# Second experts: gate and up products from half-precision high and low parts, and the routing weights spread by one product

## The chip, the cores and the metric

One core of a Trainium2 chip runs the whole program. The metric is the time of one execution on the device in microseconds (us). TensorE multiplies matrices, VectorE (DVE) and ScalarE (ACT) do elementwise work out of PSUM and SBUF, GpSimd (POOL) does elementwise work on SBUF, SyncE (SP) issues the DMAs. Each has its own queue of instructions and they meet at semaphores.

## The reference

Two layers on x of 8 x 256 tokens of 128 numbers, each a cross attention and an expert layer. Cut to what the change touches, the last expert layer:

```
logits = xf @ gate_weight.T                 # xf: 2048 x 128 (layer-normed), 32 experts
scores = sigmoid(logits)
... # 4 of 8 groups by their best score + bias, then the 6 best experts of those
combine = scores of the 6 / their sum * 2.5, else 0        # 2048 x 32
def expert_step(acc, inp):                  # for each of 32 experts
    gu, dn, c = inp
    g = xf @ gu[:I].T                       # I = 64
    u = xf @ gu[I:].T
    o = silu(g) * u @ dn.T
    return acc + c[:, None] * o
shared = (silu(xf @ shared_gate_w.T) * (xf @ shared_up_w.T)) @ shared_down_w.T     # 128 wide
x = x + tanh(g_ffn[1]) * (routed + shared)
```

Every token goes through every expert with the weight `combine`, which is zero for most.

## The kernel before

The program is a row of blocks, each with a queue per engine written out by hand; a block ends when all its engines have. Nothing is ordered by a scheduler. The last three are the second attention, `block_route1` and the product loop of `block_experts1`. The attention isn't changed, but is where rows for operations like the new ones come from.

`block_route1` (L1783): SyncE issues the loads of the router's weights and bias, and then, by `load_experts` (L1903), those of gate, up and down weights and of `spread`, all on one queue. VectorE norms x, TensorE turns it (L780), ScalarE and VectorE copy the turned x from PSUM to `xT` (L1829, L1838), TensorE makes the logits (L1822), ScalarE the sigmoid (L1831). The routing that follows is a chain of 38 VectorE instructions from L1842 to L1879, each waiting for the one before; the last writes `combine`. GpSimd has nothing in this block.

`block_experts1` (L1882): two experts of 64 make one pair of 128 columns; 16 pairs and the shared expert make N = 17 turns. TensorE turns `combine` into PSUM (L1922), ScalarE casts it to half precision `c_hi` (L1962), VectorE takes the rest into `c_lo` (L1974). Then for each of four stretches of 512 tokens ("a pass") and each turn p:

- `up(blk, p)`: gate product (L1934) and up product (L1935), both in float, and the turn's routing weights spread over its 128 columns by two half-precision products, 33 rows of `c_hi` (L1937) and 32 rows of `c_lo` (L1938) against `spread`. Three PSUM banks a turn, two sets of them.
- ScalarE: silu of the gate bank (L1968). VectorE: times the up bank (L1979), times the spread weights (L1986), which gives `inner`.
- `down(blk, p)`: four float products `inner` by down weights (L1947), added up in one bank over all 17 turns. At the end of a pass VectorE adds it to x (L1990).

Of the kernel before, what the change touches and what calls it, by code (L numbers as in the profile page):

```python
# [23 lines left out]
ACT = mybir.ActivationFunctionType  # L24
AX = mybir.AxisListType
F32 = mybir.dt.float32
F16 = mybir.dt.float16
# [3 lines left out]
P = 128  # L31
# [5 lines left out]
TOK = B * T  # L37
# [3 lines left out]
BANK = 512  # L41
# [10 lines left out]
F0 = 256  # L52
X1, I1 = 32, 64
PAIRS = X1 * I1 // P
GR, KEEP, TOP = 8, 4, 6
SCALE1 = 2.5
UB = H * TT
# [1727 lines left out]
                        query_lo(it + 3)  # L1785

def block_route1(nc, m, s, dram, load_experts):

    normed, turned, xt_act, xt_dve = (s.sem(f"r1_{n}") for n in ("normed", "turned", "xt_act", "xt_dve"))  # L1790
    logits_done, sig_done, steps, loaded = (s.sem(f"r1_{n}") for n in ("logits", "sig", "steps", "loaded"))
    with ExitStack() as stack:
# [15 lines left out]
        with nc.Block() as block:  # L1808
            @block.sync
            def _(sp):  # L1810
                sp.dma_start(wg[:, :], dram["wg1"]).then_inc(loaded, 16)
                sp.dma_start(bias[:, :], dram["expert_bias"].to_broadcast([P, X1])).then_inc(loaded, 16)
                load_experts(sp)

            @block.tensor
            def _(pe):
                pe_turn_x(nc, pe, m, normed, turned)
                pe.wait_ge(xt_act, 1)
                pe.wait_ge(xt_dve, 1)
                pe.wait_ge(loaded, 32)  # L1820
                for k in range(NT):
                    ins = nc.tensor.matmul(lg[:, k, :], m.xT[:, k * P:(k + 1) * P], wg[:, :], start=True, stop=True)  # L1822
                ins.then_inc(logits_done, 1)

            @block.scalar
            def _(act):
                ln_scalar(nc, act, m, s, 4)
                act.wait_ge(turned, 1)
                nc.scalar.copy(m.xT[:, 0:TOK // 2], m.psS[:, 0:TOK // 2]).then_inc(xt_act, 1)  # L1829
                act.wait_ge(logits_done, 1)  # L1830
                nc.scalar.activation(score[:, :, :], lg, ACT.Sigmoid).then_inc(sig_done, 1)  # L1831

            @block.vector
            def _(dve):
# [47 lines left out]
def block_experts1(nc, m, s, dram):  # L1882

    N = PAIRS + 1
    KB = BANK // P
    loaded, weights_turned, weights_ready, mixed = (s.sem(f"e1_{n}") for n in ("loaded", "turned", "ready", "mixed"))
    projected, silu_done = s.sem("e1_projected"), s.sem("e1_silu")  # L1890
    inner_done, out_full, added = (s.from_one(f"e1_{n}") for n in ("inner_done", "out_full", "added"))
    with ExitStack() as stack:
        def sb(name, shape, dt=F32):
            return stack.enter_context(nc.sbuf_tensor(name, shape, dt))

        wgate, wup, wdown = (sb(n, [P, N, P]) for n in ("e1_gate", "e1_up", "e1_down"))
        spread = sb("e1_spread", [X1 + 1, N, P], F16)
        c_hi, c_lo = sb("e1_c_hi", [X1 + 1, TOK], F16), sb("e1_c_lo", [X1, TOK], F16)
        silu, prod, inner = (sb(f"e1_{n}", [P, 2, BANK]) for n in ("silu", "prod", "inner"))
        prime(nc, s)  # L1900

        def load_experts(sp):

            for dst, src in ((wgate, dram["e1_gate"]), (wup, dram["e1_up"]), (wdown, dram["e1_down"]),
                             (spread, dram["spread"])):
                sp.dma_start(dst[:, :, :], src).then_inc(loaded, 16)

        block_route1(nc, m, s, dram, load_experts)

        def turn(blk, p):  # L1910
            return blk * N + p

        banks = [(m.psS[:, 0:BANK], m.psS[:, BANK:2 * BANK], m.psT[0][:, :]),
                 (m.psS[:, 2 * BANK:3 * BANK], m.psS[:, 3 * BANK:4 * BANK], m.psT[1][:, :])]

        with nc.Block() as block:
            @block.tensor
            def _(pe):
                pe.wait_ge(loaded, 64)  # L1920
                for k in range(NT):
                    ins = nc.tensor.transpose(m.psS[0:X1, k * P:(k + 1) * P], m.combine[:, k, :], m.ident[:, :])  # L1922
                ins.then_inc(weights_turned, 1)
                pe.wait_ge(weights_ready, 3)

                def up(blk, p):
                    n = turn(blk, p)
                    gate, upper, weight = banks[p % 2]
                    if p >= 2:
                        pe.wait_ge(inner_done, 1 + n - 1)  # L1930
                    else:
                        pe.wait_ge(inner_done, 1 + blk * N)
                    x = m.xT[:, bass.ds(blk * BANK, BANK)]
                    nc.tensor.matmul(gate, wgate[:, p, :], x, start=True, stop=True)  # L1934
                    nc.tensor.matmul(upper, wup[:, p, :], x, start=True, stop=True)  # L1935
                    tokens = bass.ds(blk * BANK, BANK)
                    nc.tensor.matmul(weight, spread[:, p, :], c_hi[:, tokens], start=True, stop=False)  # L1937
                    nc.tensor.matmul(weight, spread[0:X1, p, :], c_lo[:, tokens],  # L1938
                                     start=False, stop=True).then_inc(projected, 1)

                def down(blk, p):
                    pe.wait_ge(inner_done, 1 + turn(blk, p) + 1)
                    if p == 0:
                        pe.wait_ge(added, 1 + blk)
                    for k in range(KB):

                        ins = nc.tensor.matmul(m.psO[:, k * P:(k + 1) * P], inner[:, p % 2, k * P:(k + 1) * P],  # L1947
                                               wdown[:, p, :], start=(p == 0 and k == 0), stop=(p == N - 1),
                                               skip_group_check=True)
                    ins.then_inc(out_full, 1)  # L1950

                with pe.Fori(0, TOK // BANK) as blk:
                    up(blk, 0)
                    for p in range(N):
                        if p + 1 < N:
                            up(blk, p + 1)
                        down(blk, p)

            @block.scalar
            def _(act):  # L1960
                act.wait_ge(weights_turned, 1)
                nc.scalar.copy(c_hi[0:X1, :], m.psS[0:X1, :]).then_inc(weights_ready, 1)  # L1962
                with act.Fori(0, TOK // BANK) as blk:
                    for p in range(N):
                        n = turn(blk, p)
                        act.wait_ge(projected, n + 1)

                        nc.scalar.activation(silu[:, p % 2, :], banks[p % 2][0], ACT.Silu).then_inc(silu_done, 1)  # L1968

            @block.vector  # L1970
            def _(dve):
                nc.vector.memset(c_hi[X1:X1 + 1, :], 1.0).then_inc(weights_ready, 1)
                dve.wait_ge(weights_ready, 2)
                nc.vector.tensor_tensor(c_lo[:, :], m.psS[0:X1, :], c_hi[0:X1, :], ALU.subtract).then_inc(weights_ready, 1)  # L1974
                with dve.Fori(0, TOK // BANK) as blk:
                    for p in range(N):
                        n = turn(blk, p)
                        dve.wait_ge(silu_done, n + 1)
                        nc.vector.tensor_tensor(prod[:, p % 2, :], banks[p % 2][1], silu[:, p % 2, :],  # L1979
                                                ALU.mult).then_inc(mixed, 1)  # L1980
                        dve.wait_ge(mixed, n + 1)
                        if p >= 2:
                            dve.wait_ge(out_full, 1 + n - 1)
                        else:
                            dve.wait_ge(out_full, 1 + blk * N)
                        nc.vector.tensor_tensor(inner[:, p % 2, :], banks[p % 2][2], prod[:, p % 2, :],  # L1986
                                                ALU.mult).then_inc(inner_done, 1)
                    dve.wait_ge(out_full, 1 + turn(blk, N))
                    xs = m.x[:, bass.ds(blk * KB, KB), :]
                    nc.vector.scalar_tensor_tensor(xs, m.psO[:, :].rearrange("p (k d) -> p k d", d=E),  # L1990
                                                   m.gates[:, 3:4], xs, ALU.mult, ALU.add).then_inc(added, 1)
                dve.wait_ge(added, 1 + TOK // BANK)
# [137 lines left out]

def spread():

    out = np.zeros((X1 + 1, PAIRS + 1, P), np.float16)
    for e in range(X1):
        out[e, e // 2, e % 2 * I1:(e % 2 + 1) * I1] = 1
    out[X1, PAIRS] = 1
    return out

def pairs(routed, shared):  # L2140

    return np.concatenate([routed.reshape(PAIRS, P, E), shared[None]]).transpose(2, 0, 1)

# [47 lines left out]
```

## Time and profile before

| what | value |
| --- | --- |
| time, median of 3 runs (lowest, highest) | 3115.65 us (3114.22, 3116.72) |
| the profiled execution's own time, its span | 3115.4 us, 3113.2 us |
| TensorE clock, mean over the span | 0.936 of full |
| busy: TensorE, VectorE, ScalarE, GpSimd | 89%, 65%, 46%, 43% |
| sigmoid ends, last routing step ends | 2834.6, 2853.7 us |
| expert loop, first product to last VectorE step | 2862.2 to 3106.9 us |

A busy share is an average over stages with different limits, so the stage of the change is read by itself. Times in the rows count from the span's start. PE is the matmul, PEld the weight load, which can run beside it. A matmul's record is longer than its turn, since its end lies over the next one's start; what a product costs in a row of them is the distance from start to start.

### The profile page before, as it was taken

To read this page: it belongs to the slowest core of one execution; us is meant where nothing else is said; L and a number is where in the kernel's file an instruction comes from. 1 tells how busy PE (TensorE), PEld (TensorE's weight loads), DVE (VectorE), ACT (ScalarE), POOL (GpSimd) and SP (SyncE) were. 2 spreads that over 40 slices of the span, in tenths; PEclk is the share of its full clock that TensorE was granted. 3 is DMA by queue.
4 is the path that set the end of the run, shared out by engine and by line. 5 is a ranking of instruction groups with operands and counts; after the bars stand their busy time and mean duration, and the time that the engine had idled before them with its cause. 6 is when DMAs were issued, how large, how long until landed. Compare 5 with 4: busy or idle time off the path is not lost. (4 is left out here: it accounts for less than half of the span.)

```text
span 3113.2 us, 82961 instructions
## 1 busy us (share of the span) xinstructions
PE 2757.0 (89%) x32642; PEld 1621.3 (52%) x32642; DVE 2009.5 (65%) x6463; ACT 1447.2 (46%) x2237; POOL 1341.4 (43%) x1205
## 2 busy tenths in 40 slices
PE   4679999999953947999999999999999999994998
PEld 3423333333442734666666666666666666663544
DVE  3468888888644347667676666767676667634443
ACT  2347777777600323544545546455464554441111
POOL 2000000000000014787887878878788788780000
PEclk8789999999955968999999999999999999996999
DMA  5521111111000020000000000000000000001000
GB/s 152 151 66 24 25 25 23 23 24 26 8 27 0 0 78 19 7 18 13 7 24 7 17 12 7 23 7 18 12 7 18 12 9 7 5 2 46 0 0 13
DMA packets 109735, 75.07 MB, mean 24 GB/s; under 512 B 43921, under 2 KB 101721, under 8 KB 108862
## 3 DMA queue, kind: packets, MB, share of 16 engines
q1 hardware_dynamic: 109374, 70.02, 8.1%
q8 instruction: 255, 4.18, 0.5%
q14 instruction: 106, 0.87, 0.1%
HBM read 56.56 MB, written 13.43 MB: 22 GB/s over the span
## 5 line engine op out<-in xcount | busy, mean ns | idle before, releaser
L1442 ACT ACTIVATE a_probs<-psS 128x1024 f32<-128x1024 f32 (+1 forms) x448 | 431.7, 964 | 630.3 <-PE psS L1323 626.3
L627 ACT ACTIVATE a_probs<-psS 128x1024 f32<-128x1024 f32 (+2 forms) x512 | 443.6, 866 | 208.5 <-PE psS L568 208.2
L1759 POOL TENSOR_TENSOR a_acc<-a_acc,a_probs 128x512 f32<-128x512 f32 x320 | 406.9, 1272 | 226.5 <-ACT a_probs L1442 223.6
L1765 POOL MEMSET a_shut<- 128x3328 f16 x1 | 2.9, 2872 | 1089.7 <-POOLq L1124 1089.7
L1346 PE MATMUL psX<-a_probs,a_values 128*64 128x256 f32 x3328 | 445.6, 385 | 1.4
L654 DVE CUSTOM_DVE_ANT_0 a_junk<-psT,a_mask 128x384 f16<-128x384 f32 (+1 forms) x683 | 378.3, 573 | 61.9 <-PE psT L544 42.0
L1761 POOL TENSOR_TENSOR a_acc<-a_acc,a_probs 128x512 f32<-128x512 f32 x320 | 406.6, 1271 | 25.1
L1603 DVE CUSTOM_DVE_ANT_0 a_junk<-psT,a_mask 128x400 f16<-128x400 f32 (+1 forms) x514 | 282.5, 573 | 154.9 <-PE psS L1298 87.1
L1603 DVE CUSTOM_DVE_ANT_0 a_junk<-psS,a_mask 128x400 f16<-128x400 f32 (+1 forms) x510 | 280.7, 573 | 149.8 <-PE psT L1298 86.6
L1346 PEld LDWEIGHTS psX<-a_probs,a_values 128*64 128x64 f32 x3328 | 224.2, 137 | 104.9 <-issue 24.2
L1733 POOL TENSOR_TENSOR a_klo<-a_kt,a_khi 128x400 f16<-128x400 f32 (+1 forms) x256 | 242.3, 946 | 20.7 <-ACT a_khi L1494 20.7
L1323 PE MATMUL psS<-a_qhi,a_khi 64*128 64x256 f16 x1664 | 232.2, 276 | 8.0 <-ACT a_probs L1442 7.5
L579 PE MATMUL psX<-a_probs,a_values 128*9 128x256 f32 x3072 | 238.0, 382 | 1.0 <-ACT xn L632 1.0
L1323 PE MATMUL psS<-a_lowT,a_shut 64*128 64x256 f16 x1664 | 227.8, 270 | 0.0
L1323 PE MATMUL psS<-a_qlo,a_khi 64*128 64x256 f16 x1664 | 227.8, 270 | 0.0
L1323 PE MATMUL psS<-a_qhi,a_klo 64*128 64x256 f16 x1664 | 227.6, 270 | 0.0
L654 DVE CUSTOM_DVE_ANT_0 a_junk<-psX,a_mask 128x384 f16<-128x384 f32 (+1 forms) x341 | 195.1, 572 | 32.5 <-PE psX L544 15.1
L544 PE MATMUL psT<-a_keys,a_queries 64*128 64x384 f16 (+1 forms) x683 | 183.9, 336 | 18.2 <-DMA a_fold<-in_fold 16.4
L556 PE MATMUL psS<-a_mask_t,a_stackq 64*32 64x512 f16 (+1 forms) x4096 | 196.9, 349 | 0.0
L568 PE MATMUL psS<-a_queries,a_keys 64*128 64x256 f16 x1664 | 187.4, 277 | 1.3 <-DMA a_queries<-a_lowest 1.1
L1323 PEld LDWEIGHTS psS<-a_qhi,a_khi 64*128 64x128 f16 x1664 | 80.6, 93 | 147.8 <-issue 105.4
L1494 ACT CAST a_khi<-a_kt 128x400 f16<-128x400 f32 (+1 forms) x256 | 134.1, 524 | 33.1 <-DVE a_kt L1638 33.1
(317 smaller groups left out, 5645.5 us busy)
## 6 DMA issues: line engine op xcount, KB each, us to landing
a_kd<-p_kst SPq DMA_DIRECT2D x24, 416.0 KB, 3.1
a_wq<-in_wq SPq DMA_DIRECT2D x64, 128.0 KB, 2.1
a_keys<-a_kd SPq DMA_DIRECT2D x96, 75.0 KB
p_ctx<-in_ctx SPq DMA_DIRECT2D x8, 768.0 KB
a_ctx<-in_ctx SPq DMA_DIRECT2D x8, 768.0 KB
a_queries<-a_lowest SPq DMA_DIRECT2D x256, 0.5 KB, 2.0
p_mask_raw<-in_mask_t SPq DMA_DIRECT2D x16, 224.0 KB, 4.4
a_queries<-a_qd SPq DMA_DIRECT2D x64, 52.0 KB
```

What stands on the lines that cost most here:

```text
L556: nc.tensor.matmul(m.psS[32 * q:32 * q + 32, o:o + len(cs) * T], stackq[r, :], w.mask_t[r, at[0]:at[-1] + 1:step, :], start=True, stop=Fal ...
L568: ins = nc.tensor.matmul(m.psS[:, o:o + T], keys[r, 4 * buf + hh, key_cols(cs[x])], queries[r, buf, hh, :], start=False, stop=True, skip_g ...
L579: ins = nc.tensor.matmul(psO[o:o + VW, :], w.values[:, b, PROB_ORDER[at], h, :], probs[:, n % 2, at, :], start=(at < 4), stop=False, skip_ ...
L627: nc.scalar.activation(dst, src, ACT.Exp).then_inc(exp_done, 1)
L654: nc.vector.tensor_tensor_reduce(junk[:, (8 * n + i) % 3, 0:PIECE[j]], psA[(8 * n + i) % 3][:, 0:PIECE[j]], mask[:, t, j, 0:PIECE[j]], 1.0 ...
L1323: return nc.tensor.matmul(m.psS[:, o:o + T], keys[r, cols], queries[r, :], start=(first and x == 0), stop=False, skip_group_check=True)
L1346: ins = nc.tensor.matmul(w.sums[n % 2][64 * hd:64 * hd + 64, 0:T], w.values[:, n % 2, c, 64 * hd:64 * hd + 64], w.probs[:, k % RING1, 2 * ...
L1442: nc.scalar.activation(dst, src, ACT.Exp).then_inc(exp_done, 1)
L1603: nc.vector.tensor_tensor_reduce(w.junk[:, bank_of(name), 0:width], src[:, 0:width], w.mask[:, n // PER_BATCH % 2, o:o + width], 1.0, LOWE ...
L1733: nc.gpsimd.tensor_tensor(w.klo[:, n % KEPT1, o:o + width], w.kt[:, o:o + width], w.khi[:, n % KEPT1, o:o + width], ALU.subtract).then_inc ...
L1759: nc.gpsimd.tensor_tensor(acc, acc, src[:, :, 0, :], ALU.add).then_inc(sum_step, 1)
L1761: nc.gpsimd.tensor_tensor(acc, acc, src[:, :, 1, :], ALU.add).then_inc(sum_done, 1)
```

## The change

Gate and up products are made of half-precision high and low parts: high x high, high weights x low x, low weights x high x, added up in PSUM, three products in place of one in float. The parts are made during the routing: GpSimd multiplies the gate and up weights by 64 in place, ScalarE casts gate weights, up weights and `xT` to half precision, GpSimd subtracts each from its source. Silu scales by 1/64, and VectorE's first product has the factor 1/64 as a third operand. `c_hi` and `c_lo` are stacked in one tensor of 65 rows, and `spread` has 65 rows to match, so one product spreads them. TensorE waits for the low parts ahead of turning `combine`.

```diff
@@ block_route1
+            @block.gpsimd
+            def _(pool):
+                scale_experts(pool)
...
                 nc.scalar.activation(score[:, :, :], lg, ACT.Sigmoid).then_inc(sig_done, 1)
+                act.wait_ge(xt_dve, 1)
+                high_parts(act)
@@ block_experts1
+        def scale_experts(pool):
+            pool.wait_ge(loaded, 64)
+            for src in (wgate, wup):
+                nc.gpsimd.tensor_scalar(src[:, :, :], src[:, :, :], W1_SCALE, None, ALU.mult).then_inc(scaled, 1)
+            for i, (lo, src, hi) in enumerate(((gate_lo, wgate, gate_hi), (up_lo, wup, up_hi), (x_lo, m.xT, x_hi))):
+                pool.wait_ge(high, i + 1)
+                nc.gpsimd.tensor_tensor(lo[:], src[:], hi[:], ALU.subtract).then_inc(low, 1)
+
+        def high_parts(act):
+            act.wait_ge(scaled, 2)
+            for hi, src in ((gate_hi, wgate), (up_hi, wup), (x_hi, m.xT)):
+                nc.scalar.copy(hi[:], src[:]).then_inc(high, 1)
...
                 pe.wait_ge(loaded, 64)
+                pe.wait_ge(low, 3)
...
-                    nc.tensor.matmul(gate, wgate[:, p, :], x, start=True, stop=True)
-                    nc.tensor.matmul(upper, wup[:, p, :], x, start=True, stop=True)
-                    nc.tensor.matmul(weight, spread[:, p, :], c_hi[:, tokens], start=True, stop=False)
-                    nc.tensor.matmul(weight, spread[0:X1, p, :], c_lo[:, tokens],
-                                     start=False, stop=True).then_inc(projected, 1)
+                    for out, hi, lo in ((gate, gate_hi, gate_lo), (upper, up_hi, up_lo)):
+                        nc.tensor.matmul(out, hi[:, p, :], x_hi[:, tokens], start=True, stop=False)
+                        nc.tensor.matmul(out, hi[:, p, :], x_lo[:, tokens], start=False, stop=False)
+                        nc.tensor.matmul(out, lo[:, p, :], x_hi[:, tokens], start=False, stop=True)
+                    nc.tensor.matmul(weight, spread[:, p, :], c_both[:, tokens], start=True, stop=True).then_inc(projected, 1)
...
-                        nc.scalar.activation(silu[:, p % 2, :], banks[p % 2][0], ACT.Silu).then_inc(silu_done, 1)
+                        nc.scalar.activation(silu[:, p % 2, :], banks[p % 2][0], ACT.Silu,
+                                             scale=1.0 / W1_SCALE).then_inc(silu_done, 1)
...
-                        nc.vector.tensor_tensor(prod[:, p % 2, :], banks[p % 2][1], silu[:, p % 2, :],
-                                                ALU.mult).then_inc(mixed, 1)
+                        nc.vector.scalar_tensor_tensor(prod[:, p % 2, :], banks[p % 2][1], 1.0 / W1_SCALE,
+                                                       silu[:, p % 2, :], ALU.mult, ALU.mult).then_inc(mixed, 1)
```

TensorE's queue in the loop before, from the second turn's products to the third's (L1934 gate, L1935 up, L1937 and L1938 the spread, L1947 down):

```order
L1934 MATMUL psS<-xT,e_gate 128x512
L1935 MATMUL psS<-xT,e_up 128x512
L1937 MATMUL psT<-e_c_hi,e_spread 128x512
L1938 MATMUL psT<-e_c_lo,e_spread 128x512
L1942 REGISTER_ALU
L1944 REGISTER_ALU
L1947 MATMUL psX<-e_down,e_inner 128x128 x4
```

The same place of the changed kernel (L1961 to L1963 are the three products of high and low parts, L1964 the spread, L1972 down):

```order
L1961 MATMUL psS<-e_x_hi,e_gate_hi 128x512
L1962 MATMUL psS<-e_x_lo,e_gate_hi 128x512
L1963 MATMUL psS<-e_x_hi,e_gate_lo 128x512
L1961 MATMUL psS<-e_x_hi,e_up_hi 128x512
L1962 MATMUL psS<-e_x_lo,e_up_hi 128x512
L1963 MATMUL psS<-e_x_hi,e_up_lo 128x512
L1964 MATMUL psT<-e_c_both,e_spread 128x512
L1967 REGISTER_ALU
L1969 REGISTER_ALU
L1972 MATMUL psX<-e_down,e_inner 128x128 x4
```

Six products stand where two stood, and one where two stood; down is where it was. GpSimd's queue before ends with the attention; in the changed kernel this is behind it, in the block of the routing:

```order
L1922 ISA
L1922 TENSOR_SCALAR e_gate<-e_gate 128x2176
L1922 TENSOR_SCALAR e_up<-e_up 128x2176
L1925 TENSOR_TENSOR e_gate_lo<-e_gate,e_gate_hi 128x2176
L1925 TENSOR_TENSOR e_up_lo<-e_up,e_up_hi 128x2176
L1925 TENSOR_TENSOR e_x_lo<-xT,e_x_hi 128x2048
```

All of it is new: GpSimd had no instruction there. ScalarE gets its three casts directly behind the sigmoid.

## Rows read from the trace of the kernel before

**Rows 1.** Stages (expert passes 1, 2): length, busy us (count) by engine, clock, DMA.
```profile
2862.17:2926.30 64.13, 63.07 (x238) 31.02 (x239) 23.52 (x34) 11.44 (x18) 0.00 (x0) 0.93 0.00 1
2926.30:2986.10 59.80, 58.75 (x240) 29.85 (x239) 24.26 (x35) 11.43 (x18) 0.00 (x0) 1.00 0.00 0
```
**Rows 2.** Timeline, one turn: start us, length us, engine, line, operation, shapes, idle before.
```profile
2879.33 1.02 PE L1934 MATMUL psS<-xT,e_gate 128*128 x2
2880.20 1.02 PE L1935 MATMUL psS<-xT,e_up 128*128 x2
2881.15 0.39 PE L1937 MATMUL psT<-e_c_hi,e_spread 33*128 x1
2881.47 0.39 PE L1938 MATMUL psT<-e_c_lo,e_spread 32*128 x1
2881.78 1.16 PE L1947 MATMUL psX<-e_down,e_inner 128*128 128x128 f32 x8
2881.89 0.60 ACT L1968 ACTIVATE e_silu<-psS 128x512 f32<-128x512 f32 x1 [2.85 <-PE psT L1938]
...
2882.78 1.02 PE L1934 MATMUL psS<-xT,e_gate 128*128 x2
2883.24 0.69 DVE L1986 TENSOR_TENSOR e_inner<-psT,e_prod 128x512 f32<-128x512 f32 x1
```
**Rows 3.** Timeline, second attention: half-precision products of 64, then 128 rows.
```profile
2002.34 0.33 PE L1298 MATMUL psS<-a_khi,a_qhi 64*128 64x400 f16 x2
2002.61 0.23 PE L1275 MATMUL psT<-a_wv,a_chi 128*128 128x128 f16 x1
2002.62 0.10 PEld L1276 LDWEIGHTS psT<-a_wv,a_chi 128*128 128x128 f16 x1
2002.67 0.22 PE L1276 MATMUL psT<-a_wv,a_chi 128*128 128x128 f16 x1
```
**Rows 4.** Timeline: four float transposes, then a half-precision product.
```profile
1299.87 0.66 PE L1249 MATMUL psS<-ident,a_ctx 128*128 128x128 f32 x4
1300.37 0.22 PE L1275 MATMUL psS<-a_wv,a_chi 128*128 128x128 f16 x1
```
**Rows 5.** Timeline, end of the first pass.
```profile
2922.79 0.39 PE L1938 MATMUL psT<-e_c_lo,e_spread 32*128 x1
...
2925.31 1.16 PE L1947 MATMUL psX<-e_down,e_inner 128*128 128x128 f32 x8 [1.05 <-DVE e_inner L1986]
...
2926.64 0.75 DVE L1990 SCALAR_TENSOR_TENSOR x<-psX,gates,x 128x512 f32 x1 [1.38 <-PE psX L1947]
```
**Rows 6.** DMA, 2812 to 2862 in 40 slices of 1.25 us.
```profile
GB/s 0 0 15 85 225 418 446 418 418 418 359 14 0 7 0 0 0 0 0 0 0 0 0 0 0 0 0 0 0 0 0 0 0 0 0 0 0 0 0 0
```
**Rows 7.** Groups by line and shape: count, busy us, mean ns of one, idle before.
```profile
L1522 ACT CAST a_wk<-a_probs 128x1024 f16<-128x1024 f32 x2 | 2.0, 1037 | 0.0
L1727 POOL TENSOR_TENSOR a_clo<-a_c,a_chi 128x512 f16<-128x512 f32 x24 | 27.1, 1128 | 4.9 <-ACT a_c L1477 4.9
L1721 POOL TENSOR_TENSOR a_wk<-a_probs,a_wk 128x1024 f16<-128x1024 f32 x2 | 4.2, 2118 | 16.7 <-ACT a_wv L1522 16.7
```
**Rows 8.** Timeline, routing.
```profile
2834.01 0.60 ACT L1831 ACTIVATE r_score<-psX 128x512 f32<-128x512 f32 x1 [6.00 <-PE psX L1822]
...
2836.09 1.23 DVE L1849 TENSOR_TENSOR r_first<-r_best 128x1024 f32<-128x1024 f32 x1
...
2853.27 0.43 DVE L1879 TENSOR_SCALAR combine<-r_score 128x512 f32<-128x512 f32 x1
```
**Rows 9.** Timeline, second attention: GpSimd and VectorE at once, two places.
```profile
1153.68 4.19 POOL L1721 TENSOR_TENSOR a_wk<-a_probs,a_wk 128x1024 f16<-128x1024 f32 x2 [16.70 <-ACT a_wv L1522]
...
1156.39 1.52 DVE L1592 SCALAR_TENSOR_TENSOR a_moved<-a_mv,a_rstd 128x13 f32<-128x13 f32 x1
...
1264.69 1.26 POOL L1763 TENSOR_TENSOR a_acc<-a_acc,a_probs 128x512 f32<-128x512 f32 x1
...
1265.16 0.82 DVE L1584 TENSOR_SCALAR a_var<-a_mv 128x13 f32<-128x13 f32 x1
```

More of the change, by code:

```diff
@@ L54 @@
 PAIRS = X1 * I1 // P
+W1_SCALE = 64.0
 GR, KEEP, TOP = 8, 4, 6
@@ L1785, in _, with block_route1 @@
                         query_lo(it + 3)
-def block_route1(nc, m, s, dram, load_experts):
+def block_route1(nc, m, s, dram, load_experts, scale_experts, high_parts):
     normed, turned, xt_act, xt_dve = (s.sem(f"r1_{n}") for n in ("normed", "turned", "xt_act", "xt_dve"))
@@ L1896, in block_experts1 @@
         wgate, wup, wdown = (sb(n, [P, N, P]) for n in ("e1_gate", "e1_up", "e1_down"))
-        spread = sb("e1_spread", [X1 + 1, N, P], F16)
-        c_hi, c_lo = sb("e1_c_hi", [X1 + 1, TOK], F16), sb("e1_c_lo", [X1, TOK], F16)
+        spread = sb("e1_spread", [2 * X1 + 1, N, P], F16)
+        c_both = sb("e1_c_both", [2 * X1 + 1, TOK], F16)
+        gate_hi, gate_lo, up_hi, up_lo = (sb(n, [P, N, P], F16) for n in ("e1_gate_hi", "e1_gate_lo", "e1_up_hi", "e1_up_lo"))
+        x_hi, x_lo = sb("e1_x_hi", [P, TOK], F16), sb("e1_x_lo", [P, TOK], F16)
+        scaled, high, low = s.sem("e1_scaled"), s.sem("e1_high"), s.sem("e1_low")
         silu, prod, inner = (sb(f"e1_{n}", [P, 2, BANK]) for n in ("silu", "prod", "inner"))
@@ L1906, in load_experts @@
                 sp.dma_start(dst[:, :, :], src).then_inc(loaded, 16)
-        block_route1(nc, m, s, dram, load_experts)
+        def scale_experts(pool):
[9 more added lines that the diff above has]
+                nc.scalar.copy(hi[:], src[:]).then_inc(high, 1)
+        block_route1(nc, m, s, dram, load_experts, scale_experts, high_parts)
         def turn(blk, p):
@@ L1932, in up @@
                         pe.wait_ge(inner_done, 1 + blk * N)
-                    x = m.xT[:, bass.ds(blk * BANK, BANK)]
-                    nc.tensor.matmul(gate, wgate[:, p, :], x, start=True, stop=True)
-                    nc.tensor.matmul(upper, wup[:, p, :], x, start=True, stop=True)
                     tokens = bass.ds(blk * BANK, BANK)
-                    nc.tensor.matmul(weight, spread[:, p, :], c_hi[:, tokens], start=True, stop=False)
-                    nc.tensor.matmul(weight, spread[0:X1, p, :], c_lo[:, tokens],
-                                     start=False, stop=True).then_inc(projected, 1)
+                    for out, hi, lo in ((gate, gate_hi, gate_lo), (upper, up_hi, up_lo)):
[3 more added lines that the diff above has]
+                    nc.tensor.matmul(weight, spread[:, p, :], c_both[:, tokens], start=True, stop=True).then_inc(projected, 1)
                 def down(blk, p):
@@ L1961, in _ @@
                 act.wait_ge(weights_turned, 1)
-                nc.scalar.copy(c_hi[0:X1, :], m.psS[0:X1, :]).then_inc(weights_ready, 1)
+                nc.scalar.copy(c_both[0:X1, :], m.psS[0:X1, :]).then_inc(weights_ready, 1)
                 with act.Fori(0, TOK // BANK) as blk:
@@ L1966, in _ @@
                         act.wait_ge(projected, n + 1)
-                        nc.scalar.activation(silu[:, p % 2, :], banks[p % 2][0], ACT.Silu).then_inc(silu_done, 1)
+                        nc.scalar.activation(silu[:, p % 2, :], banks[p % 2][0], ACT.Silu,
+                                             scale=1.0 / W1_SCALE).then_inc(silu_done, 1)
             @block.vector
             def _(dve):
-                nc.vector.memset(c_hi[X1:X1 + 1, :], 1.0).then_inc(weights_ready, 1)
+                nc.vector.memset(c_both[2 * X1:2 * X1 + 1, :], 1.0).then_inc(weights_ready, 1)
                 dve.wait_ge(weights_ready, 2)
-                nc.vector.tensor_tensor(c_lo[:, :], m.psS[0:X1, :], c_hi[0:X1, :], ALU.subtract).then_inc(weights_ready, 1)
+                nc.vector.tensor_tensor(c_both[X1:2 * X1, :], m.psS[0:X1, :], c_both[0:X1, :], ALU.subtract).then_inc(weights_ready, 1)
                 with dve.Fori(0, TOK // BANK) as blk:
@@ L2131, in spread @@
 def spread():
-    out = np.zeros((X1 + 1, PAIRS + 1, P), np.float16)
+    out = np.zeros((2 * X1 + 1, PAIRS + 1, P), np.float16)
     for e in range(X1):
-        out[e, e // 2, e % 2 * I1:(e % 2 + 1) * I1] = 1
-    out[X1, PAIRS] = 1
+        out[e::X1, e // 2, e % 2 * I1:(e % 2 + 1) * I1] = 1
+    out[2 * X1] = 0
+    out[2 * X1, PAIRS] = 1
     return out
```

## Prediction

> **What bounds the kernel now.** I read the stage table first. The last stage, the second set of experts, is four equal passes over 512 tokens. TensorE is busy 58.75 of 59.80 us in a pass at full clock, VectorE 24.3 and ScalarE 11.4 [rows 1]. The first pass takes 64.13 us, with the clock at 0.93 of full: its start runs at the lower of the two levels. The four passes go from 2862.17 to 3106.20, 244.0 us. So what is worth anything here is TensorE's time per pair of experts.
>
> Then one pair in the timeline [rows 2]. From gate product to gate product (2879.33 to 2882.78) it takes 3.45 us: gate 0.87, up 0.95, first spread 0.32, second spread 0.31, down with its weight loads 1.00. Nothing in it is a wait for another engine: the silu and the two VectorE steps of the pair end at 2883.93, and TensorE by then is in the next pair's products. A float product of 512 columns is 0.87, four times 0.216. The two spread products have half-precision operands and also stream 512 columns, yet take 0.32 and 0.31. They have 33 and 32 rows beside neighbours of 128. The same extra stands elsewhere: from the two 64-row products of 400 columns to the 128-row one is 0.27 [rows 3], where 400 columns at the same rate are 0.17. So a change of the number of rows in use costs about 0.10, and each pair has three of them (128 to 33, 33 to 32, 32 to 128). The Trainium skill (TensorEngine Tiling (Array Packing), "Key Properties") says that changing the tiling mode drains the engine; this trace agrees, 0.10 each.
>
> **The products.** Per pair the change takes out two float products and one of the two spread products and puts in six half-precision products; the remaining spread has 65 rows. Price of a new one: half-precision products with 128 rows and 128 columns and fresh weights each follow one another at 0.06 (2002.61, 2002.67) with loads of 0.10 [rows 3], that is, the load is hidden. Four times 0.056 is 0.22, and a quarter of the float product is 0.216. I take 0.216. Going from float to half precision with 128 rows on both sides costs nothing extra: the last of the four transposes starts at 1300.26, the next half-precision product at 1300.37, 0.11 later, the transposes' own step [rows 4]. I take the three mode changes as gone, since 65 rows don't fit a half: this is the step with the least behind it (if 65 rows were a mode of their own, 0.2 a pair). The down products keep their 8 steps of 0.112, but the first load, now open (0.10, in the 1.00), hides: 0.90.
>
> New TensorE time of a pair: 7 x 0.216 + 0.90 = 2.41 us. Before: 3.445.
>
> **Is the other chain now late?** From the start of a pair's last product until the down product can start is 2.52 us through silu, product and product (2922.79 to 2925.31, where TensorE had nothing else to do) [rows 5]. In the new order, between these two stand spread 0.216, the preceding down 0.90, six products 1.29: the next spread starts after 2.41 and ends after 2.62. The load of the down weights can start at 2.52 and takes 0.10: 2.62. So TensorE and the chain end together. The multiply by 1/64 turns a two-operand step into a three-operand one. The nearest row, a three-operand step on the same shape out of PSUM, is 0.75 against 0.69 [rows 5]; the chain would be 2.58. As the down product of pair p waits for this chain and two pairs share it, a pair costs (2.68 + 2.19)/2 = 2.435 then. Range 2.41 to 2.44; I take 2.42. Scaling inside silu costs ScalarE nothing I can see (0.60 a call, idle for 2.85 before it).
>
> **A pass.** At its start TensorE runs two pairs' products before the first down; with them short, it now waits there. In us from the first product: last product of pair 0 starts 1.30, its down product 1.30 + 2.52 = 3.82 (pair 1's products end at 3.0: a new wait of 0.8), 1.00 for it, six products 1.29: spread of pair 2 at 6.1, down of pair 1 at 6.3. Then 14 steps of 2.42 to the down of pair 15: 40.2. The last pair's spread started 0.22 before, its down waits until 2.52 after that: 42.5, and takes 1.0: 43.5. Before, 59.80. Three warm passes save 16.3 each. The first also has the cold start. Before, it costs 64.13 - 59.80 = 4.3. Unless the clock rises at another time, the same 9 us of half speed now hold the same loss less the waits of the pass's start, 3.4. Passes after: 4 x 43.5 + 3.4 = 177.4. Saved: 244.0 - 177.4 = 66.6.
>
> **The splitting, during the routing.** GpSimd scales gate and up weights, ScalarE casts three tensors, GpSimd subtracts three times. GpSimd has nothing else then. The expert weights arrive at 418 GB/s, all by about 2826 [rows 6], gate and up by my count of these slices at 2822.6. The scaling's price on GpSimd isn't in the trace: at nothing it ends at 2822.6, at the rate of the two-operand steps below 4.4 each, at 2831.4. Either is before 2834.6, when the sigmoid's end lets ScalarE start its casts, so I cost it at nothing; it would need to pass 6 us each to matter. Casts: 1.04 for 1024 elements [rows 7], so about 2.0 for 2176. The first ends at 2836.7. GpSimd's subtractions: 1.13 for 512 and 2.12 for 1024 elements [rows 7], 1.93 ns an element: 4.35, 4.35 and 4.10, sum 12.8. Alone they would end at 2849.5, ahead of VectorE's routing chain, whose last step starts at 2853.27 [rows 8]: hidden.
>
> But they aren't alone. A VectorE step of 13 elements, with two inputs in SBUF, started at 1156.39 and took 1.52 us; GpSimd's subtractions ran from 1153.68 for 4.19, so it ended as the second of them did, 1157.9. A one-input step of 13 elements that started 1265.16 took 0.82, until GpSimd's step of 1264.69 + 1.26 ended [rows 9]. VectorE stood still until the GpSimd instruction was over. The Trainium skill says so (SBUF — State Buffer, "Who interferes with whom"): a port pair shared by the two is an exclusive lock for the whole instruction, for VectorE steps with two SBUF inputs or in the two-port mode. The rows agree, and by the rule most of the routing's steps contend, for they are of this kind.
>
> So: at 2836.7 VectorE is in a 1.23 step from 2836.09 [rows 8]; GpSimd's first subtraction gets its turn at 2837.3 and holds up the next VectorE step by 4.35. That step runs, the next subtraction follows, and so on, three turns: VectorE is held up for the whole 12.8 us. All that follows waits for it: transposes, spreading, products. If GpSimd only got its turn at steps that don't contend (the reductions, the sorting), some 1.2 us each would be overlapped: 9.3. I take 12.8; the bounds are 0 and 12.8.
>
> The rest (wait for the low parts ahead of the transposes, the wider table, the memset of another row) stands beside or behind things that end later: GpSimd ends by 2852.6 in this plan, VectorE at 2866.5. Nothing.
>
> **Sum.** -66.6 + 12.8 = -53.8. The profiled execution took 3115.4 (span 3113.2), close to the median 3115.65, so **3062 us**.
>
> **Rivals.**
> 1. VectorE isn't held up in the routing (the few cases above were chance meetings, or the lock is given up within long steps). Against it: every row I have of a meeting. Time 3062 - 12.8 = 3049. Chance 0.13.
> 2. The chain of silu and two products bounds the loop: it is as long as TensorE's part already. If it is 2.75 instead of 2.52 (a longer last product of 65 rows, the 0.75 step, one more handover), a pair is (2.85 + 2.19)/2 = 2.52, 0.10 x 64 = 6.4 more, and 1.8 more at the passes' ends: 3070. Chance 0.14.
> 3. Changes of precision or of rows are paid after all, 0.1 twice a pair: 2.62 for a pair, 0.20 x 64: 3075. Chance 0.06. The same time comes if GpSimd's scaling is several times slower than its subtractions.
> 4. Weights are not loaded under a product that uses the same rows. Then every product costs 0.32: 7 x 0.32 + 1.00 = 3.24, 0.2 x 68 = 14 saved, 12.8 lost: 3114. The Trainium skill has this rule (TensorE: Matmul & The Clock Gate, "The mechanism": the load overlaps only when the row group differs). The trace contradicts it: loads of 0.10 with the same 128 rows, products 0.056 apart. Chance 0.03.
> 5. Slower: the products run one by one, each as long as its record (0.39 for 512 columns [rows 2]) because two of three wait for the accumulation of the one before into the same bank. 7 x 0.39 + 1.00 = 3.73 a pair, 0.28 x 68 = 19 more, plus 12.8: 3147. It decides from 3.26 a pair up, 0.32 a product. Against it: the 128-row products at 0.056 add up in one place too, with records of 0.22. Chance 0.03.
>
> The forecast itself has 0.61. Its own range is 3056 to 3067. The range for 8 in 10 goes over rivals 1 and 2 and to the edge of 3: 3047 to 3077. This kernel can tell 0.2% from no change, 6 us. Faster 0.94 (all but 4 and 5), the same 0.03 (4), slower 0.03 (5).
>
> **What would show it.** In the profile after: a pair at 2.4 to 2.45, products 0.216 apart; no 0.10 before and after the spread product; a wait of about 1 us for VectorE's second product at each pass's end, and a new one of 0.8 at its start; and in the routing three steps of 128x1024 that take 5.6 us instead of 1.23, while GpSimd's three subtractions run. If the routing still takes 19 us from sigmoid to its last step, rival 1 holds; if TensorE waits for VectorE in each pair, rival 2; if weight loads start only as a product starts, 3 or 4.

## The result, and the profile after

The changed kernel takes 3064.05 us (median of 4, 3061.78 to 3065.07) against 3114.93 before; ratio 0.9841, 95% interval 0.9822 to 0.986. A second session gave 0.9834 (0.9818 to 0.985). The forecast was 3062.

The profiled execution has a span of 3062.3, 50.9 less. By stretches, in us:

| stretch | before | after | difference |
| --- | --- | --- | --- |
| up to the sigmoid's end (changed in it: a larger `spread` load, and GpSimd's start) | 2834.6 | 2836.6 | +2.0 |
| sigmoid's end to the last routing step's end | 19.1 | 34.5 | +15.4 |
| from there to the first product of the loop | 8.5 | 8.8 | +0.3 |
| the loop, to the last VectorE step's end | 244.75 | 176.08 | -68.7 |

**The loop.** The stage table of the changed kernel, the first two of its four passes (columns as in [rows 1]; the third is like the second):

```profile
2879.87:2924.73 44.86, 43.05 (x255) 27.41 (x256) 23.51 (x34) 11.43 (x18) 0.00 (x0) 0.96 0.00 1
2924.73:2968.11 43.38, 41.44 (x257) 26.97 (x255) 24.26 (x35) 11.43 (x18) 0.00 (x0) 1.00 0.00 0
```

A warm pass takes 43.38 where it took 59.80 [rows 1]. One turn of it, from the timeline:

```profile
2887.75 1.05 PE L1972 MATMUL psX<-e_down,e_inner 128*128 128x128 f32 x8
2887.95 0.60 ACT L1993 ACTIVATE e_silu<-psS 128x512 f32<-128x512 f32 x1 [2.64 <-PE psT L1964]
2888.58 0.69 DVE L2005 SCALAR_TENSOR_TENSOR e_prod<-psS,e_silu 128x512 f32<-128x512 f32 x1 [1.82 <-ACT e_silu L1993]
2888.64 0.38 PE L1961 MATMUL psS<-e_x_hi,e_gate_hi 128*128 x1
2888.86 0.38 PE L1962 MATMUL psS<-e_x_lo,e_gate_hi 128*128 x1
2889.07 0.38 PE L1963 MATMUL psS<-e_x_hi,e_gate_lo 128*128 x1
2889.29 0.38 PE L1961 MATMUL psS<-e_x_hi,e_up_hi 128*128 x1
2889.30 0.69 DVE L2012 TENSOR_TENSOR e_inner<-psT,e_prod 128x512 f32<-128x512 f32 x1
2889.50 0.38 PE L1962 MATMUL psS<-e_x_lo,e_up_hi 128*128 x1
2889.72 0.38 PE L1963 MATMUL psS<-e_x_hi,e_up_lo 128*128 x1
2889.93 0.38 PE L1964 MATMUL psT<-e_c_both,e_spread 65*128 x1
2890.16 1.05 PE L1972 MATMUL psX<-e_down,e_inner 128*128 128x128 f32 x8
```

From down to down it is 2.41 us where it was 3.45 [rows 2]. Each product comes 0.215 after the last, the spread product of 65 rows too, with no gap on either side. Down takes 0.89 to the next product, 0.11 less than before. VectorE's second product ends at 2889.99, the load of the down weights starts at 2890.05, and TensorE's down begins at 2890.16, straight behind the spread product. So TensorE doesn't wait here, but only just.

Each pass begins with the new wait for VectorE (0.70 us, forecast 0.8). Spread of turns 0 and 1, and the down of turn 0:

```profile
2926.03 0.38 PE L1964 MATMUL psT<-e_c_both,e_spread 65*128 x1
...
2927.54 0.38 PE L1964 MATMUL psT<-e_c_both,e_spread 65*128 x1
...
2928.62 1.15 PE L1972 MATMUL psX<-e_down,e_inner 128*128 128x128 f32 x8 [0.70 <-DVE e_inner L2012]
```

**The routing.** The timeline from the first routing step on shows where 15.4 us went; it answers to [rows 8]:

```profile
2829.28 5.71 POOL L1922 TENSOR_SCALAR e_gate<-e_gate 128x2176 f32<-128x2176 f32 x1 [24.14 <-DMA e_spread<-in_spread]
...
2834.96 5.71 POOL L1922 TENSOR_SCALAR e_up<-e_up 128x2176 f32<-128x2176 f32 x1
...
2836.59 4.39 DVE L1849 TENSOR_TENSOR r_masked<-r_score,r_bias 128x512 f32<-128x512 f32 x1 [6.32 <-ACT r_score L1836]
...
2841.73 1.23 DVE L1856 TENSOR_TENSOR r_first<-r_best 128x1024 f32<-128x1024 f32 x1
...
2842.85 4.30 POOL L1925 TENSOR_TENSOR e_gate_lo<-e_gate,e_gate_hi 128x2176 f16<-128x2176 f32 x1 [2.18 <-ACT e_gate_hi L1931]
2842.99 5.24 DVE L1857 TENSOR_TENSOR r_level<-r_best 128x1024 f32<-128x1024 f32 x1
...
2847.11 5.28 POOL L1925 TENSOR_TENSOR e_up_lo<-e_up,e_up_hi 128x2176 f16<-128x2176 f32 x1
2848.27 5.20 DVE L1858 TENSOR_TENSOR r_level<-r_level,earlier 128x1024 f32<-128x1024 f32 x1
...
2852.36 5.03 POOL L1925 TENSOR_TENSOR e_x_lo<-xT,e_x_hi 128x2048 f16<-128x2048 f32 x1
2853.51 4.96 DVE L1860 TENSOR_TENSOR r_first<-r_first,r_level 128x1024 f32<-128x1024 f32 x1
```

The two engines take turns: GpSimd's subtraction, then the one VectorE step that waited for it, then the next subtraction, whose record is longer by 1.0 us (5.28 against 4.30), because it in turn waits. Three steps of 1.23 (the first of them too, [rows 8]) take 5.24, 5.20 and 4.96: 11.7 us too many. The first step of the routing is 4.39 instead of 0.69: it ends at 2840.98, just behind the second scaling (2834.96 + 5.71 = 2840.67).

### The profile page after: what moved, and what is told of

It is laid out like the page before. It is cut to its first block and busy times, and to the rows that moved or that the text cites. A ratio compares the mean times of both kernels' runs of the same rounds, so it can differ in the third digit from the quotient of the medians.

```text
span 3062.3 us, 83109 instructions
## 1 busy us (share of the span) xinstructions
PE 2682.0 (88%) x32710; PEld 1612.8 (53%) x32710; DVE 2023.6 (66%) x6463; ACT 1451.6 (47%) x2240; POOL 1367.4 (45%) x1210
```

## The experiments

All ratios are to the kernel before, timed beside them. From one profile to the next the second attention, which none of these kernels touches, ended up to 12 us earlier or later, so a time by itself is good to some 5 us. Stretches inside a trace repeat better: a pass at the full clock agrees to 0.02 us between two profiles of the changed kernel. Two stretches vary: the loop's start, with the moment at which the clock rises (the whole loop was 176.08 and 176.56), and the first routing step, with how far GpSimd's scaling has got.

**GpSimd writes, but doesn't read.**

```diff
-                nc.gpsimd.tensor_tensor(lo[:], src[:], hi[:], ALU.subtract).then_inc(low, 1)
+                nc.gpsimd.memset(lo[:], 0.0).then_inc(low, 1)
```

> GpSimd's three subtractions are replaced by memsets of the same three tensors: it writes them but reads nothing, so the low parts are zero. The scaling stays. Theory (a GpSimd instruction that reads SBUF holds up VectorE steps with two SBUF inputs for its whole length): the three routing steps of 128x1024 that took 5.0 to 5.2 us go back to 1.23, and only the first step (L1849, 4.39 us while GpSimd scales) stays long; sigmoid's end to the routing's last step falls from 34.5 to about 22.8 us, the time from 3064 to about 3052. Rival (any GpSimd instruction holds VectorE up, writing ones too): memsets of some 1.9 us each still lengthen steps, together by up to 5.7: about 3058. Rival (it was not GpSimd's subtractions): no change, 3064.

Measured: 3049.79 us, 0.9801 (0.9786 to 0.9816); sigmoid's end to routing's end 23.45 us. From the timeline:

```profile
2828.63 5.71 POOL L1922 TENSOR_SCALAR e_up<-e_up 128x2176 f32<-128x2176 f32 x1
...
2829.80 4.85 DVE L1849 TENSOR_TENSOR r_masked<-r_score,r_bias 128x512 f32<-128x512 f32 x1 [6.29 <-ACT r_score L1836]
...
2836.49 1.91 POOL L1925 MEMSET e_gate_lo<- 128x2176 f16 x1 [2.15 <-ACT e_gate_hi L1931]
2836.66 1.23 DVE L1857 TENSOR_TENSOR r_level<-r_best 128x1024 f32<-128x1024 f32 x1
2837.92 1.23 DVE L1858 TENSOR_TENSOR r_level<-r_level,earlier 128x1024 f32<-128x1024 f32 x1
...
2840.25 1.80 POOL L1925 MEMSET e_x_lo<- 128x2048 f16 x1
...
2841.69 0.44 DVE L1862 TENSOR_SCALAR r_keep<-r_keep 128x128 f32<-128x128 f32 x1
```

The steps with two SBUF inputs are 1.23 again under a GpSimd instruction that only writes. The last row is another case: this one-input step is 0.23 in the kernel before, and here 0.44; it ends at 2842.13, just behind the memset (2842.05). The routing's 23.45 are the 19.09 of before, 4.16 for the first step and 0.2 for this one; that is 0.6 over the forecast, mostly because the first step met more of the scaling than in the changed kernel's profile. The Trainium skill (SBUF — State Buffer, "Who interferes with whom") separates the two just so: steps with two SBUF inputs contend with GpSimd's reads only, the two-port mode with both. The rows of two-input steps agree; the one-input step fits too, but whether it ran in the two-port mode no trace shows.

**No scaling.**

```diff
-            for src in (wgate, wup):
-                nc.gpsimd.tensor_scalar(src[:, :, :], src[:, :, :], W1_SCALE, None, ALU.mult).then_inc(scaled, 1)
...
-            act.wait_ge(scaled, 2)
+            act.wait_ge(loaded, 64)
```

> The scaling of gate and up weights by 64 is left out (factor 1 everywhere), so GpSimd only subtracts, and ScalarE casts right behind the sigmoid. Theory: the first routing step, 4.39 us now, goes back to 0.69, and the three subtractions still hold up three later steps by 4.35, 4.35 and 4.10 less what is overlapped: sigmoid to routing's end 34.5 - 3.7 = 30.8 us, time about 3061. Rival (the scaling held nobody up, the first step was long for another reason): first step stays at 4.4, 3064.

Measured: 3056.15 us, 0.9813 (0.9798 to 0.9828); routing 30.78 us. The first step is 0.69 again, the three others 5.21, 5.20 and 4.96. The routing is 3.7 shorter, as forecast. The time fell by some 8; the rest lies ahead of the routing and isn't the experiment's: in this profile the block began 4.3 us earlier, and the logits took 4.5 us at a mean granted clock of 0.81, where they took 5.5 at 0.64.

**The splitting on ScalarE and VectorE.** GpSimd gets nothing; the factor goes into the cast and into VectorE's subtraction. Gate and up weights get a semaphore of their own, so that the casts wait for these two loads alone, and TensorE waits for the low parts behind the turning of combine, not ahead of it.

```diff
+            for hi, src in ((gate_hi, wgate), (up_hi, wup)):          # ScalarE, ahead of the sigmoid
+                nc.scalar.activation(hi[:], src[:], ACT.Copy, scale=W1_SCALE).then_inc(high, 1)
+            nc.scalar.copy(x_hi[:], m.xT[:]).then_inc(high, 1)
...
+            for i, (lo, src, hi) in enumerate(((gate_lo, wgate, gate_hi), (up_lo, wup, up_hi))):   # VectorE, ahead of the routing
+                dve.wait_ge(high, i + 1)
+                nc.vector.scalar_tensor_tensor(lo[:], src[:], W1_SCALE, hi[:], ALU.mult, ALU.subtract).then_inc(low, 1)
...
+                nc.vector.tensor_tensor(x_lo[:], m.xT[:], x_hi[:], ALU.subtract).then_inc(low, 1)   # VectorE, while TensorE turns combine
```

> The whole result is computed, but GpSimd does nothing in the routing: ScalarE casts with the factor 64 before the sigmoid, while TensorE makes the logits; VectorE takes both weights' low parts in its idle stretch before the sigmoid (6.3 us long) and x's low part in its idle stretch while TensorE turns the routing weights. Theory: three VectorE steps of about 2.3 us, all in idle stretches, and nothing held up: sigmoid to routing's end 19.1 us again, and all of the 15.4 us come back: about 3049. Rival (the splitting is as much work on any engine, and the 6.8 us on VectorE come onto the path): 3056. Rival (what was lost in the routing was not GpSimd's doing): 3064.

Measured: 3048.18 us, 0.9796 (0.9782 to 0.9809); routing 19.08 us. In this profile the sigmoid came 1.8 us later after the block's start than in the changed kernel's. Most of that is the clock: the logits took 7.0 us here, at a granted clock of 0.50 (1.2 GHz) throughout, and 5.5 there, at 0.64. They took 7.0 at 0.50 in the profile of the two spread products below as well, which leaves this block as it is in the changed kernel.

```profile
2825.46 2.43 DVE L1928 SCALAR_TENSOR_TENSOR e_gate_lo<-e_gate,e_gate_hi 128x2176 f16<-128x2176 f32 x1 [2.14 <-ACT e_gate_hi L1921]
...
2827.80 2.42 DVE L1928 SCALAR_TENSOR_TENSOR e_up_lo<-e_up,e_up_hi 128x2176 f16<-128x2176 f32 x1
2829.14 1.28 ACT L1835 ACT_TABLE_LOAD   x1
2830.47 0.60 ACT L1835 ACTIVATE r_score<-psX 128x512 f32<-128x512 f32 x1
```

VectorE's steps lie in its idle stretch and cost nothing; the same subtraction is 2.4 us here, 4.3 on GpSimd.

**The same, with x's cast behind the sigmoid**, and the changed kernel once more beside it.

> The changed kernel itself once more, beside the next one on the same chip, because the stages that no kernel here touches (the second attention, ahead of the routing) began up to 8 us earlier or later from one profile to the next. By every theory 0.984 of the kernel before, and from the sigmoid's end to the routing's last step 34.5 us.

> As the version with the splitting on ScalarE and VectorE, but x's cast comes behind the sigmoid. There the sigmoid's table load ended at 2830.42, as late as the logits (2830.43), which took 7.0 us in that run and 5.5 in others. Theory (the cast in front makes the sigmoid late by up to 1.4 us when the logits are fast): table load ends 1.9 us earlier, the sigmoid follows the logits at once, and all of the changed kernel's loss in the routing is back: 15.4 us below the changed kernel's time, ratio to before 0.979. Rival (the sigmoid waits for the logits anyway): the same as that version, 14 below.

Measured: the changed kernel 3064.3 us, 0.9834 (0.9818 to 0.985), with 35.3 us for the routing instead of 34.5, its first step 5.18 long. The new version 3042.38 us, 0.9778 (0.9762 to 0.9795). It has the routing at 19.09 us, block start to sigmoid's end at 20.47 as before (22.24 in the version above), the first product 8.5 after the routing. So the whole loss is back: 17 us by ratios, 16.2 + 0.3 by the stretches of the two traces (the medians differ by 22, and in these profiles the sigmoid ended 5.2 us earlier in the new version). It beats both kernels and computes the whole result. Against the version above its intervals overlap; that moving the cast gives the sigmoid anything is seen in the trace only, and there the logits ran at the faster clock (5.5 us, not 7.0), so it isn't shown.

**The spread product alone**, on the kernel before: `c_hi` and `c_lo` stacked, one product of 65 rows; all else as before.

> The kernel before with one part of the change only: one spread product of 65 rows instead of two of 33 and 32 rows. Gate and up products stay in float, no splitting. Theory (each change of the number of rows costs 0.10 us, and one product of 0.216 goes): a pair costs 4 x 0.43 + 0.216 + 0.90 = 2.84 us instead of 3.445, a pass about 50.2 instead of 59.8, the time 3115 - 38.5 = about 3076. Rival (only the product itself goes, 0.32, row changes stay): 3115 - 22 = 3093.

Measured: 3074.63 us, 0.9887 (0.9871 to 0.9904). A pass takes 50.15 us. One turn:

```profile
2869.94 1.05 PE L1945 MATMUL psX<-e_down,e_inner 128*128 128x128 f32 x8
2870.83 1.02 PE L1934 MATMUL psS<-xT,e_gate 128*128 x2
2871.69 1.02 PE L1935 MATMUL psS<-xT,e_up 128*128 x2
2872.55 0.38 PE L1937 MATMUL psT<-e_c_both,e_spread 65*128 x1
2872.77 1.05 PE L1945 MATMUL psX<-e_down,e_inner 128*128 128x128 f32 x8
```

2.83 a turn: of the 1.04 that the change takes off, 0.62 are the spread's. The median is 36 us lower; the forecast was 38.5.

**The change without the spread's part**: two products, 33 and 32 rows.

```diff
-                    nc.tensor.matmul(weight, spread[:, p, :], c_both[:, tokens], start=True, stop=True).then_inc(projected, 1)
+                    nc.tensor.matmul(weight, spread[:, p, :], c_hi[:, tokens], start=True, stop=False)
+                    nc.tensor.matmul(weight, spread[0:X1, p, :], c_lo[:, tokens], start=False, stop=True).then_inc(projected, 1)
```

> The changed kernel with that one part undone: spread by two products of 33 and 32 rows, as before; six half-precision products and the splitting stay. Theory (three changes of rows at 0.10 and a product of 0.216 come back): a pair 3.02 us instead of 2.41, a pass about 52.6 instead of 43.4, time about 3064 + 37 = 3101. Rival (only a product of 0.216 comes back): 2.63, about 3079.

Measured: 3103.3 us, 0.997 (0.9959 to 0.9981). A pass takes 52.8, a turn 3.02:

```profile
2911.81 0.38 PE L1962 MATMUL psS<-e_x_lo,e_up_hi 128*128 x1
2912.03 0.38 PE L1963 MATMUL psS<-e_x_hi,e_up_lo 128*128 x1
2912.34 0.39 PE L1964 MATMUL psT<-e_c_hi,e_spread 33*128 x1
2912.66 0.39 PE L1965 MATMUL psT<-e_c_lo,e_spread 32*128 x1
2912.97 1.16 PE L1974 MATMUL psX<-e_down,e_inner 128*128 128x128 f32 x8
2913.97 0.38 PE L1961 MATMUL psS<-e_x_hi,e_gate_hi 128*128 x1
```

Two products 0.22 apart, then 0.31, 0.32, 0.31 around the row changes, and 1.00 for down again. The pass was forecast at 52.6 and the time at 3101. The clock rose 12.4 us after the loop's first product here, later than in any other profile.

Where the 0.10 goes, the rows of the weight loads show. Two of the kernel before (the turn of [rows 2]), then one of the changed kernel (the turn above):

```profile
2881.14 0.09 PEld L1937 LDWEIGHTS psT<-e_c_hi,e_spread 33*128 33x128 f16 x1 [0.76 <-issue]
2881.46 0.09 PEld L1938 LDWEIGHTS psT<-e_c_lo,e_spread 32*128 32x128 f16 x1 [0.23 <-issue]
...
2889.72 0.10 PEld L1964 LDWEIGHTS psT<-e_c_both,e_spread 65*128 65x128 f16 x1
```

With 65 rows the load starts together with the product ahead of it (2889.72) and lies under it. With 33 or 32 rows it starts 0.31 after the start of the product ahead (2881.46 behind 2881.15), when that product's 0.216 are over, and its own product follows within 0.01. Whether TensorE first has to run empty, or only the load comes late, these rows don't tell apart.

**The 65-row product twice**: one more product, no row change.

> The changed kernel with the 65-row spread product made twice (so the routing weights count double). Theory (a product more with the same rows costs 0.216 and no row change): a pair 2.63 us, time 3064 + 14.7 = about 3079. Rival (a second spread product costs 0.32 whatever its rows): 3086.

Measured: 3078.56 us, 0.9894 (0.9877 to 0.991), a pass 46.8. The second comes 0.22 after the first, from the timeline:

```profile
2912.20 0.38 PE L1964 MATMUL psT<-e_c_both,e_spread 65*128 x1
2912.42 0.38 PE L1965 MATMUL psT<-e_c_both,e_spread 65*128 x1
2912.64 1.05 PE L1974 MATMUL psX<-e_down,e_inner 128*128 128x128 f32 x8
```

This and the last experiment give TensorE the same number of products. A turn is 2.62 here and 3.02 there: 0.40 are three row changes of 0.10 and the open load of the first down weights, by rows alone. A pass differs by 6.0, not 17 x 0.40 = 6.8, mostly since the slower one waits less for VectorE at the pass's start (0.18 against 0.48) and end (1.05 against 1.25).

**Four products in place of six.**

```diff
-                        nc.tensor.matmul(out, hi[:, p, :], x_lo[:, tokens], start=False, stop=False)
-                        nc.tensor.matmul(out, lo[:, p, :], x_hi[:, tokens], start=False, stop=True)
+                        nc.tensor.matmul(out, hi[:, p, :], x_lo[:, tokens], start=False, stop=True)
```

> Low weights x high x is left out of gate and up: four half-precision products a pair in place of six, 0.43 us less for TensorE. Theory (the chain of silu and two VectorE steps, 2.52 us and a weight load, ends together with TensorE in the changed kernel, so that it is the bound from here on): a pair (2.62 + 1.76)/2 = 2.19 us, not 1.98; a pass 39.4 instead of 43.4; time about 3048, with TensorE waiting for VectorE's second step in nearly every pair. Rival (TensorE alone bounds the loop): 1.98 a pair, 3064 - 29 = 3035.

Measured: 3045.21 us, 0.9785 (0.9769 to 0.9801), a pass 39.47 (forecast 3048 and 39.4). Three turns' down products:

```profile
2899.95 1.16 PE L1971 MATMUL psX<-e_down,e_inner 128*128 128x128 f32 x8 [0.16 <-DVE e_inner L2011]
...
2902.03 1.06 PE L1971 MATMUL psX<-e_down,e_inner 128*128 128x128 f32 x8
...
2904.33 0.94 PE L1971 MATMUL psX<-e_down,e_inner 128*128 128x128 f32 x6 [0.16 <-DVE e_inner L2011]
```

4.38 for two turns, 2.19 for one, as forecast; the wait for VectorE is in every second turn, where I had expected it in nearly every one. 34 products fewer a pass, 7.3 us of TensorE's time, brought 3.9. The chain of silu and two products is the bound from here on.

## Why the prediction was right, step by step

- **Products at 0.216, loads hidden.** Right: from 2900 on, from each of the six products to the next one is 0.21 or 0.22 everywhere in the trace. The rule that a load can't lie under a product of the same rows (rival 4) fails here: the loads of 128 rows overlap. It is the load across a change of rows that doesn't.
- **Row changes cost 0.10 each and are gone with 65 rows.** This was the step with least behind it. Right: 0.31 to 0.32 with 33 and 32 rows against 0.22 with 65, in experiments of its own. What the prediction gave no words to: with the better hidden down load this is more than half of what the change wins, 0.62 of 1.04 a turn. Without it the products take 26.9 us off the loop (217.8 in that profile; 28 in the passes, less 1 for the late clock), and the routing gives 13.1 of them back. That alone would be 0.996; in that profile the sigmoid ended 6.4 us later than before, and the runs gave 0.997.
- **TensorE and the chain end together.** Right, as closely as the rows can tell. The three-operand step is 0.69, not 0.75, so the lower end of 2.41 to 2.44 held. The experiment with four products shows that the formula for the chain as the bound also holds.
- **Pass 43.5.** 43.38, with the new wait at its start (2.59 from the first spread product to its down, forecast 2.52). The cold start cost 1.5, not 3.4: by the trace's record the granted clock rose from 1.2 to 2.4 GHz 3.3 us after the first product, where before it rose 8.8 us after (in the two versions without GpSimd 5.4). I had assumed the same 9 us; nothing in the profile before says how that moves. It isn't a property of the change either: in the second profile of the same changed kernel it rose after 5.9 us. So 1.9 of the 2.1 us by which the loop beat the forecast hang on the moment of this rise, which no profile here explains. The loop gained 68.7, forecast 66.6.
- **GpSimd holds VectorE up.** Right in kind, in the taking of turns, and nearly in size: VectorE lost 4.0, 4.0 and 3.7, together 11.7 where I had 12.8; each is some 0.3 under the subtraction's own length. The writing-only experiment shows that it is the reading that locks.
- **The scaling at nothing.** Wrong, by 3.7 us. I let it start when gate and up weights are there, at 2822.6, and priced it at 4.4 at most, so ending at 2831.4. It was 5.71 each, a one-input instruction dearer than a two-input one, and it started at 2829.3. I had taken the wait for 64 as passed with gate and up; it counts four loads of one semaphore, the down weights and the spread table with them. So the second scaling ran into the first routing step. The start was the larger miss, 6.7 us against 1.3 a piece: with the loads all in at about 2826 [rows 6], even 4.4 us each end at 2834.8, behind the sigmoid. The prediction had asked for over 6 us each "to matter", which held only for a start at 2822.6; at 5.71 it mattered. How much it costs depends on where they meet: 1.4 to 4.5 in the six profiles that have it (3.7 in the changed kernel's first); without scaling nothing.
- **The sum.** -68.7 + 15.4 + 0.3 + 2.0 = -51.0, against -53.8. Two misses of opposite sign, the loop's 2.1 and the routing's 2.6, all but cancel, so that the total came out within 3 us is in part luck. The routing's miss is itself two, 3.7 too little for the scaling and 1.1 too much for the subtractions. The +2.0 is the drift of the attention that no kernel here explains.

Left open: what sets when the clock rises (3.3 to 12.4 us after the loop's first product over eleven profiles), why the first product comes 8.8 us behind the routing instead of 8.5, and why the untouched attention ends at other times from run to run. (Two line numbers in the text ahead are off: `block_route1` stands at L1788 and `load_experts` at L1902.)

## What to carry to other kernels

Work "on an idle engine" isn't free if that is GpSimd and VectorE is on the path: list VectorE's steps with two SBUF inputs, and count each GpSimd instruction that reads SBUF as a full stop for them (here 3.7 to 4.0 us for one of 4.1 to 4.3). ScalarE, or VectorE's own gaps, did the same work for nothing. Look also at when such work can start: a wait for a semaphore's count stands for every load that adds to it. In a tight row of products look at the number of rows each uses: stacking two small products of 33 and 32 rows into one of 65 gained more (0.62 us a turn) than making the big ones cheaper (0.42). And when TensorE's turn shrinks, compare it at once with the chain that hands its result back: here they met at 2.41 us, and the next cut was worth half.

## What the runs showed of the hardware that I had not expected

- A one-input multiply on GpSimd over 2176 float elements with a float result takes 5.71 us, the two-input subtraction with a half-precision result 4.30, a memset of the latter's tensor 1.91.
- With 65 rows a product's weight load lay under the product of 128 rows ahead of it; with 33 or 32 rows it did not, and each change cost 0.10 us.
- The same kernel's clock rose 3.3 us after the loop's first product in one profile and 5.9 us in another; the logits, 32 small products, took 4.5, 5.5 or 7.0 us at a mean granted clock of 0.81, 0.64 and 0.50.
- The lock shows on both sides: VectorE's step is long by GpSimd's rest, and GpSimd's next instruction by VectorE's step (5.28 instead of 4.30).
- A GpSimd memset, which reads nothing, still held up a one-input VectorE step (0.44 instead of 0.23), while two-input steps beside it ran at full speed.
